# Gathered-edge products of a graph network kernel: tile by tile, both feature halves together, and only the spanned columns

## What is computed

```
h = jax.nn.relu(x @ w1 + b1)
msg = ew[:, None] * h[src]
agg = jax.ops.segment_sum(msg, dst, num_segments=x.shape[0])
h = agg @ w2 + b2
return jax.nn.relu(_bn(h, g, b))
```

## Time and profile before

| | us |
|---|---|
| median of 3 runs | 4848.33 |
| lowest, highest | 4831.88, 4853.95 |
| span of the profiled execution | 5228.2 |
| TensorE busy in it | 4623.3 |
| VectorE, ScalarE, GpSimd busy in it | 2688.7, 2435.6, 2110.6 |
| granted TensorE clock, mean of the span | 0.946 |

### The profile page before, as it was taken

How to read it: one execution, slowest core, us unless ns; L and a number is a source line. 1 busy time by engine, 2 the same in 40 slices (tenths; PEclk the granted TensorE clock), 3 DMA queues, 4 the chain that set the end, 5 groups by cost and what they waited for, 6 DMA issues and landing times. The chain is left out here.

```text
span 5228.2 us, 71544 instructions
## 1 busy us (share of the span) xinstructions
PE 4623.3 (88%) x25508; PEld 3800.6 (73%) x25508; DVE 2688.7 (51%) x6606; ACT 2435.6 (47%) x4218; POOL 2110.6 (40%) x2284
## 2 busy tenths in 40 slices
PE   6778888888999579888988988649999999999999
PEld 5667777666677467776666666548888888888888
DVE  7666666566333464522222222366666666666665
ACT  4655556666211263300000000057777777777777
POOL 1466666566666456666666666630000000000000
PEclk9889999999999789999999999779999999999999
DMA  5467777566755247876666666431111111001110
GB/s 155 148 210 271 243 240 245 188 211 217 236 198 201 77 141 268 277 243 218 218 219 205 226 212 224 131 96 25 30 28 33 33 33 33 24 26 33 33 28 15
DMA packets 546618, 770.23 MB, mean 147 GB/s; under 512 B 149720, under 2 KB 441411, under 8 KB 546262
## 3 DMA queue, kind: packets, MB, share of 16 engines
q1 hardware_dynamic: 328176, 382.01, 21.7%
q0 software_dynamic: 100944, 273.96, 16.4%
q10 hardware_dynamic: 117142, 109.65, 6.5%
HBM read 605.58 MB, written 147.26 MB: 144 GB/s over the span
## 5 line engine op out<-in xcount | busy, mean ns | idle before, releaser
L1106 PE MATMUL pf<-work 128*128 128x330 f32 (+4 forms) x3528 | 1251.9, 491 | 63.3 <-DMA work<-front 31.3
L1054 POOL DMA_INDIRECT wst<-h,src_col x1040 | 1000.3, 962 | 541.9 <-issue 275.0
L1106 PEld LDWEIGHTS pf<-work 128*128 128x128 f32 x3528 | 661.0, 197 | 402.2 <-issue 220.1
L2096 DVE TENSOR_TENSOR f_hl<-f_hf,f_hh 128x1024 fp32r<-128x1024 f32 (+1 forms) x400 | 479.7, 1199 | 636.3 <-ACT f_hf L1959 636.0
L1952 ACT ACTIVATE f_hh<-f_p,f_sh,f_sc 128x512 fp32r<-128x512 f32 (+1 forms) x800 | 571.7, 768 | 395.9 <-PE f_p L2194 394.5
L1273 ACT ACTIVATE ah<-agg 128x1024 fp32r<-128x1024 f32 (+1 forms) x50 | 51.8, 1037 | 1464.2 <-DVE agg L1420 1086.6
L1138 PEld LDWEIGHTS ps<-oh,wst 128*128 128x128 f32 x4160 | 543.4, 203 | 144.5 <-issue 99.6
L1138 PE MATMUL ps<-oh,wst 128*128 128x128 f32 x4160 | 560.7, 288 | 88.6 <-issue 55.1
L1054 POOL DMA_INDIRECT f_xr<-h,src_col x518 | 497.7, 961 | 282.8 <-issue 134.0
L1054 POOL DMA_INDIRECT f_u<-h,src_col x512 | 491.1, 959 | 260.5 <-issue 136.7
L1959 ACT ACTIVATE f_hf<-f_p,f_sh,f_sc 128x512 f32<-128x512 f32 (+1 forms) x800 | 572.5, 775 | 0.0
(11 more groups left out here) (285 smaller groups left out, 7648.0 us busy)
## 6 DMA issues: line engine op xcount, KB each, us to landing
work<-h SPq DMA_DIRECT2D x216, 512.0 KB
work<-front SPq DMA_DIRECT2D x50, 924.0 KB
front<-agg ACTq DMA_DIRECT2D x12, 3300.0 KB
work<-front SPq DMA_DIRECT2D x50, 756.0 KB
work<-front SPq DMA_DIRECT2D x50, 660.0 KB
work<-front SPq DMA_DIRECT2D x50, 580.0 KB
front<-agg ACTq DMA_DIRECT2D x8, 2600.0 KB
work<-front SPq DMA_DIRECT2D x25, 832.0 KB
```

The costliest lines, as they stand in the source:

```text
L1054: g.indirect_dma_start(G[t % R], None, h_dram[layer], bass.IndirectOffsetOnAxis(ap=src_col[:, col:col + 1], axis=0)).then_inc(ga[t % R], 16)
L1106: ins = g.matmul(pF[:, k, 0:count * w].rearrange("p (s c) -> p s c", c=w), HB[a % 2][0:r, n, k * P:(k + 1) * P], x, start=b == 0, stop=b = ...
L2096: g.tensor_tensor(hlo[l][q % 2][:, :, 0:nn], hf[l][:, :, 0:nn], hhi[l][q % 2][:, :, 0:nn].bitcast(fp32), ALU.subtract).then_inc(f_lo[l], 1)
```

## The change

The gathered products of a group go tile by tile, both feature halves of a tile behind one another, in place of all tiles for the first half and then all tiles for the second. They move only the first `width` columns of the one-hot matrix and write only those of the bank. The flags that open and close the accumulation stand on the first and the last product of the group, since both halves lie in one bank. In the planner the group's products cost 16 * max(64, 8 + width * 5 / 6) in place of 16 * 111.

```diff
-            other = [16 * 111 + sum(max(224, NB * hot(layer, t)[4] * 9 // 10) for t in hot_behind(layer, q))
+            other = [16 * max(64, 8 + width(FGL[layer] + q) * 5 // 6) + sum(max(224, NB * hot(layer, t)[4] * 9 // 10) for t in hot_behind(layer, q))
                      + (560 if q > ZERO_Q[layer] else 0) for q in range(NQL[layer])]
...
-                            for k in range(KC):
-                                for t in tiles_of[q]:
-                                    if k == 0:
-                                        g.wait_ge(ga[t % R], gathered_value(layer, t))
-                                    ins = g.matmul(pS[bank_of[q]][:, k, :], G[t % R][:, k * P:(k + 1) * P], OH[t % RO],
-                                                   start=t == tiles_of[q][0], stop=t == tiles_of[q][-1])
+                            wide = width(FGL[layer] + q)
+                            for t in tiles_of[q]:
+                                g.wait_ge(ga[t % R], gathered_value(layer, t))
+                                for k in range(KC):
+                                    ins = g.matmul(pS[bank_of[q]][:, k, 0:wide], G[t % R][:, k * P:(k + 1) * P], OH[t % RO][:, 0:wide],
+                                                   start=t == tiles_of[q][0] and k == 0, stop=t == tiles_of[q][-1] and k == KC - 1)
                             ins.then_inc(g_mm, 1)
```

## The result

| | median us | lowest, highest | runs |
|---|---|---|---|
| before | 4851.69 | 4831.88, 4853.97 | 7 |
| after | 4865.43 | 4862.38, 4881.18 | 7 |

The ratio is 1.0043, 95% interval 1.0028 to 1.0058. The change makes the kernel slower, by 14 us between the medians and 21 us by the ratio. The loss is small, but the interval excludes no change. The same pair measured again in the experiments gives 1.0060 (1.0047 to 1.0073), 29 us. The forecast was 12 us. A ratio here is estimated from all runs of the two kernels and need not be the quotient of their medians.

What follows compares the result with a forecast made beforehand. TensorE and GpSimd were taken to share the bound in the two aggregates, TensorE 4.89 us a group, GpSimd 5.0. Terms 0 - 4 - 5 + 0 + 20 = +11 us on 4848 gave 4860, range 4785 to 4930.

Steps and rivals of the forecast that it cites:

- first case: Gathered products stay bound by their stationary loads, so little changes: 4860 us, own range 4826 to 4872, chance 0.52.
- Spacing of records: Gathered product records stay some 111 ns apart with 28 to 82 moving columns, because each stationary load remains: 0 us.
- The mean record 30 to 40 ns shorter: Sign expected in the profile after: the mean record of L1138, the gathered products, gets 30 to 40 ns shorter.
- The end of a group: Last narrow record ends sooner, so g_mm rises 0.04 us sooner for GpSimd: -11 us at most, taken as -4.
- The order: Fewer products behind the last gathered tile, 0.67 us sooner where TensorE waits for it: -17 us at most, taken as -5.
- fourth case: Slightly faster through the order, if less disturbed timed runs wait more often for last tiles: 35 us, 4815, chance 0.08.
- The planner: New group cost shifts units by one group or two, density kept: 0 us, bounds -10 and +10.
- The clock: TensorE's granted clock may fall as records move fewer columns, in both aggregates: bounds 0 and +85 us, taken as +20.
- second case: Slower because the clock falls more often: 36 us in layer 0's first 30 groups, 49 elsewhere; 4925 us, chance 0.28.
- The thresholds of what would show it: Mean clock under 0.75 from 179 to 430 us, or under 0.92 in the stretches behind, would tell the second case.
- third case: Faster because the load isn't the bound: records 70 ns apart, GpSimd's waits partly won; -100 us, 4750, chance 0.12.
- The excess of the profile: Profile span 379.9 us above the median, cause left open; timed runs hold 160 to 540 us of GpSimd's waits.

Runs made afterwards that it cites:

- e3: Kernel before with only the new tile-by-tile order, all 128 columns and the old planner; 5217.2 us against 5222.5, ratio 0.9999.
- e12: e3 plus six full-width products on unused data behind each of the first 28 groups of layer 0; 4846.3 us against 4845.9 before, ratio 1.0004.
- e4: Kernel before with only the planner's new cost of a group; 5225.3 us against 5222.5, ratio 1.0009.
- e8: Changed kernel with the old planner's cost of 16 * 111; 4874.7 us against 4846.3 before, ratio 1.0060.
- e5: The changed kernel measured again, nothing else altered; 4875.4 us against 4846.3 before, ratio 1.0060.
- e2: Kernel before with only the narrow columns, old order and old planner; 5243.0 us against 5222.5, ratio 1.0041.
- e9: Kernel before, unchanged, measured a third time and profiled on a faster chip; 4847.0 us against 4845.9, ratio 1.0001.
- e7: Kernel before with six of a group's 16 product records dropped, so its sums are incomplete; 4790.1 us against 4846.3, ratio 0.9889.
- e1: Kernel before, unchanged, measured and profiled again on the slower chip; 5220.7 us against 5222.5, ratio 1.0003.
- e10: e8 with all 128 columns in the whole of layer 0, narrow ones in layer 1; 4854.0 us against 4845.9 before, ratio 1.0019.
- e6: e8 with all 128 columns in the first 60 gathered groups of layer 0; 4861.1 us against 4846.3 before, ratio 1.0039.
- e11: e8 plus six full-width products on unused data behind each of the first 28 groups of layer 0; 4870.1 us against 4845.9 before, ratio 1.0055.

## Why the prediction was right, and where its steps were off

The time came out at 4865 where 4860 was forecast, within the range and within the first case's own range. The mechanism of the first case held: the spacing stayed, and the clock took a little. How near the number came is in part luck. The +20 for the clock wasn't summed up from rows but chosen between 0 and 85, two small gains that it was set against didn't come, and 36 of the 85 us stood on the first 30 groups, which lose about 1. The steps:

- **Spacing of records: right.** The 111 ns stayed (period of 4.88 to 4.89 us at 56 columns). L702's one column had told it and the transposes' 70 ns had not. The loads kept their mean of 200 ns. The rule of the Trainium skill, "TensorE: Matmul & The Clock Gate", section "LDWEIGHTS (loading the stationary operand)", gives a load's time by its stationary columns alone, 107 ns for 128. The spacing here agrees, with 107.5 to 111 ns (1.72 and 1.78 us for 16); the load records themselves are listed with some 200.
- **The mean record 30 to 40 ns shorter: wrong.** It is 283 against 285, and the median stays at 275 in L1138's rows. Only the first record of a run is shorter. I had taken a record's length to follow its columns.
- **The end of a group, -4 us: wrong.** The 0.58 us for four records of L702 and the 1.95 for sixteen were compared as if both ran on alike. In the changed kernel the last record of a run keeps its 275 ns at 56 columns, and the event of the group's end comes 289 ns after its start against 288, so g_mm doesn't rise sooner.
- **The order, -5 us: too much.** e3 has the order alone at 0.9999 on 5220 us; its interval of 4 to 5 us on either side allows a gain of 5 us only at its end. It was bounded by a count of waits that I knew only from the slower chip. There TensorE waited for gathers 25 times, on the faster ones 186 times. My fourth case rested on just this ("timed runs, less disturbed") and its premise was true. It still brought nothing: e12, with the new order on a faster chip, is at 1.0004. The likely reason, which no run isolates, is that those waits are where GpSimd leads, and a group that ends 0.67 us sooner there shortens nothing.
- **The planner, 0: right.** e4 (0.0 to 0.2%) and e8 (1.0060, as e5) bear it out.
- **The clock, +20 us: the term that carried the forecast, with the right sign, near in size, and the place wrong.** e2 shows sign and size together: columns alone, clock 0.82 to 0.66, +0.41%. But I had put 36 us of the second case's price on the first 30 groups. Their clock fell as said, 0.85 to 0.75, and cost about 1 us (150.6 us for 28 groups against 149.2). The step that failed is the price of those groups, "3.1 us a group at full clock, 6.2 at the lower one, against GpSimd's 5.0". It has the clock at the lower level all the time, and before at full clock. In fact it is at the lower level for 111 of 222 us, and before already for 67. The added 44 us cost TensorE 22 us of work, and its idle time of 222 - 171 = 51 us in that stretch of e9 has room for it. The second part, 49 us for 5% more time at the lower level in all other groups alike, was closer in size: 194 - 110 = 84 us came, 3.7% of the 2270 us of those stretches. But it took one price for groups that have two. In the last 150 groups of layer 1 some 40 us more at the lower level cost 0 to 2 us, since GpSimd sets the pace there; the loss comes from groups 28 to 188 of layer 0 and 20 to 100 of layer 1, where TensorE does.
- **The thresholds of what would show it: no good.** The first stretch has 0.75 in after, but 0.74, 0.73 and 0.66 in e5, e8 and e2, where "under 0.75" was to mean the second case; the two long stretches have 0.96 and 0.97, but the last one 0.82, and e2 has 0.92 to 0.93 where "under 0.92" was the sign. All of these lose 0.4 to 0.6%, so a low mean of the first stretch doesn't tell the second case's time.
- **The third case's price of 100 us: too high.** With 345 us taken from TensorE e7 gains 56. The timed runs hold 110 us of waits, not the 160 to 540 that I bounded, and two thirds of them go.
- **The excess of the profile.** I had left open what the 380 us are. GpSimd's waits for products are 529 us on the slower chip (e1) and 110 on the faster (e9). The 529 hold about 56 us of the ordinary 0.30 between gathers ("issue" is 548 us in 1789 places there, 604 in 1981 here). GpSimd's whole idle time before gathers is 1077 us against 714, 363 more for a time difference of 376. So nearly all of the excess shows up there, and the low bound of 160 was near.

What stays open. No kernel here changes the clock alone where TensorE sets the pace, since there it has no room for filling. That the columns cost the time is shown (e2, e10); that they do so through the clock rests on the spacing that stayed at full clock and on lower level and time going together. Open too is whether the first measurement's 0.43% and the 0.60% of the others are one value, and how much of what e6 gives back is real: its trace is 3 us ahead of e8's in the first 28 groups and 3 us in the next 32, and further ahead where the two kernels are alike.

## What to carry to other kernels

Before moving columns are cut, look whether the records' spacing follows the columns. Here each fp32 record has a load of 128 stationary columns of its own, and one, 56 or 128 moving columns cost the same 107 to 113 ns. With fewer columns at the same spacing TensorE was granted a lower clock, so such a cut can make a kernel slower. It did so where TensorE sets the pace (5.4 us for a group), not where its clock fell deepest, nor where GpSimd's 5.0 us for a group covers it. To find that out, cut two traces at the same piece of work and not at the same time. And when a profile's span and the timed median differ by per cents, first time the kernel on the chip of the profile: counts of waits don't carry over.

## What the runs showed of the hardware that I had not expected

- **Chips differ by 7.8% for this kernel**: 5222.5 us on one against 4846 on two others, and the parts of the change (e2 to e4) ran at 5217 to 5243 on the slower one. The trace of the slower one has TensorE standing still with "issue" before L1138 for 327.6 us in 615 places (e1), against 57.4 us in 228 (e9). There the records come singly or in pairs, here e1 in layer 1:

```profile
2658.86 0.39 PE L1138 MATMUL ps<-oh,wst 128*128 128x128 f32 x2
2660.25 0.27 PE L1138 MATMUL ps<-oh,wst 128*128 128x128 f32 x1 [1.00 <-issue]
2660.96 0.39 PE L1138 MATMUL ps<-oh,wst 128*128 128x128 f32 x2 [0.43 <-issue]
2662.38 0.27 PE L1138 MATMUL ps<-oh,wst 128*128 128x128 f32 x1 [1.03 <-issue]
```

  Nothing that the profile names releases them. The cause wasn't found.
- **Fewer moved columns went with a lower clock.** At the same number of records and loads (1009 and 1013 in the first stretch) the granted clock was 0.66 against 0.82 (e2 against e1). Six more full-width products for each group went with 0.90 against 0.73 (e11 against e8), but there the records rose too, from 1030 to 1386.
- **Time at the lower clock can be free.** In the last 150 groups of layer 1 it rose from 38 to 79 us, and the stretch took 756.1 us against 755.9.
- **A record's length doesn't tell its columns.** Within a run a record of 56 columns is listed with 275 ns as one of 128 is.
